# Last stage of a two-layer audio tower: top-2 experts by sorted tiles of rows instead of all eight experts for every token

## The reference

```python
logits = jnp.einsum('bsh,he->bse', x, gate_w) + gate_b
topk_vals, topk_idx = jax.lax.top_k(logits, K)                 # K = 2, E = 8
topk_weights = jax.nn.softmax(topk_vals, axis=-1)
mask = jax.nn.one_hot(topk_idx, E, dtype=topk_weights.dtype)
weights = jnp.einsum('bske,bsk->bse', mask, topk_weights)
h = jax.nn.relu(jnp.einsum('bsh,ehf->bsef', x, w1) + b1)
expert_out = jnp.einsum('bsef,efh->bseh', h, w2) + b2
return jnp.einsum('bseh,bse->bsh', expert_out, weights)
```

## Time and profile before

| what | value |
| --- | --- |
| median of three runs | 2385.1 us (2382.28 to 2393.17) |
| profiled execution, whole | 2387.96 us |
| its span, first to last instruction | 2386.1 us |
| mean granted TensorE clock | 0.944 of full speed |
| busy: PE, DVE, ACT, POOL | 86%, 66%, 45%, 32% |

### The profile page before, as it was taken

The page is one execution under the profiler, slowest core; times in us unless marked ns, Lnnn a source line. Parts: engine busy times, 40 slices in busy tenths (PEclk is TensorE's granted clock), DMA queues, the critical chain, the costliest instruction groups (busy, mean ns, idle before and its releaser), DMA issues. The chain is left out here.

```text
span 2386.1 us, 54761 instructions
## 1 busy us (share of the span) xinstructions
PE 2052.9 (86%) x20986; PEld 1812.3 (76%) x20986; DVE 1563.6 (66%) x3984; ACT 1079.6 (45%) x2700; POOL 769.3 (32%) x730
## 2 busy tenths in 40 slices
PE   6599989998726776786899999994999999999998
PEld 5497778786615676686677777773999999999998
DVE  4745665654743653556699999996666676676664
ACT  4433333422614453452666666662444444444443
POOL 0002222200055424520577777774121121121120
PEclk9899999999858897898999999997999999999999
DMA  7100100100311101100000000000000000000000
GB/s 180 37 1 12 15 11 12 15 1 2 111 42 35 30 20 35 36 16 1 3 3 3 3 3 3 3 3 1 8 8 7 13 7 7 13 7 7 13 7 14
DMA packets 80356, 44.52 MB, mean 19 GB/s; under 512 B 45800, under 2 KB 74024, under 8 KB 79752
## 3 DMA queue, kind: packets, MB, share of 16 engines
q1 hardware_dynamic: 74248, 29.53, 5.4%
q0 software_dynamic: 5888, 12.07, 1.9%
HBM read 27.20 MB, written 14.38 MB: 17 GB/s over the span
## 5 line engine op out<-in xcount | busy, mean ns | idle before, releaser
L2103 ACT ACTIVATE w<-banks,b 128x384 f32<-128x384 f32 (+1 forms) x512 | 259.5, 572 | 392.9 <-PE banks L2177 392.9
L2159 PE MATMUL banks<-w,w 128*128 128x128 f32 (+1 forms) x3072 | 364.1, 275 | 0.0
L2159 PEld LDWEIGHTS banks<-w,w 128*128 128x128 f32 (+1 forms) x3072 | 350.4, 189 | 9.1 <-issue 8.7
L1694 PE MATMUL banks<-qT,w 64*64 64x128 f32 x4608 | 272.2, 271 | 14.9 <-DVE eb L1597 12.3
L1702 PE MATMUL banks<-eb,w 64*64 64x128 f32 x4608 | 272.4, 271 | 0.7 <-DVE eb L1597 0.7
L1694 PEld LDWEIGHTS banks<-qT,w 64*64 64x64 f32 x4608 | 249.3, 133 | 29.8 <-DVE eb L1597 17.0
L2004 DVE SCALAR_TENSOR_TENSOR h<-banks,t_wt,h 128x128 f32 (+3 forms) x672 | 183.9, 343 | 115.1 <-PE banks L2159 112.4
L1702 PEld LDWEIGHTS banks<-eb,w 64*64 64x64 f32 x4608 | 249.2, 133 | 1.3 <-DVE eb L1597 1.1
L1237 POOL DMA_INDIRECT xg<-xs,rowu x184 | 179.2, 974 | 152.3 <-PE banks L1388 90.4
L1662 POOL TENSOR_TENSOR t<-eb 128x768 f32<-128x768 f32 x96 | 175.9, 1832 | 135.8 <-ACT eb L1642 123.7
L1597 DVE TENSOR_TENSOR eb<-eb,rd 128x1536 f32<-128x1536 f32 x96 | 211.7, 2205 | 1.6 <-ACT rd L1651 1.6
(11 more groups left out here) (309 smaller groups left out, 4354.4 us busy)
## 6 DMA issues: line engine op xcount, KB each, us to landing
out<-h SPq DMA_DIRECT2D x16, 320.0 KB
xs<-r_xl SPq DMA_DIRECT2D x16, 192.0 KB, 2.9
h<-in_xT SPq DMA_DIRECT2D x4, 750.0 KB, 15.0
h<-in_xT SPq DMA_DIRECT2D x4, 749.0 KB, 17.9
xg<-xs,rowu POOLq DMA_INDIRECT x184
xs<-r_xl SPq DMA_DIRECT2D x16, 128.0 KB
blocks<-NT SPq DMA_DIRECT2D x24, 48.0 KB, 1.9
D<-blocks SPq DMA_DIRECT2D x24, 48.0 KB, 2.0
```

The source lines that it names most:

```text
L1694: last = nc.tensor.matmul(lbanks(n)[place(n, hd), v, :], k.Kt[half(hd), v, :], qT[half(hd), n // NC % 2, (n % NC) * P:(n % NC + 1) * P], s ...
L2103: nc.scalar.activation(gb[u % 2][:, f, s * GW:s * GW + NFREE[s]], k.ps[:, order.bank(n), 0:NFREE[s]], ACT.Relu, bias=k.b1_1[:, 2 * e + f:2 ...
L2159: last = nc.tensor.matmul(k.psf[0:n, o:o + P], gb[u % 2][:, f, c * P:c * P + n], k.w2_1[:, 2 * e + f, :], start=(f == 0), stop=(f == 1))
```

## The change

`TailOrder` gives way to `TailPlan`, and the tail stage is written out anew, without loops. Per pair of sequences (1492 tokens, 2984 choices):

- The fronts of both sequences of the next pair are done in 15 items (`FRONT`), one in each step of the pair in hand. DVE does them in a fixed order of its own, ending in `places`; the normalisation of the attention's result moves from DVE to ACT (`norm_out`), the products with the norm's parameters move from POOL to DVE (two passes in `norm_sum`), and POOL keeps one addition (`shift`) and the roots.
- `places`: PE counts, by 13 matmuls, how many choices for each expert come ahead of each token; DVE works out from it where in a list sorted by expert each choice goes (each expert begins at a multiple of 128 rows), and which expert owns each of the 31 tiles of 128 rows.
- `send`: POOL writes the normalised tokens to that list in DRAM (`sorted_x`), by 24 indirect transfers (six chunks, two sequences, two choices).
- SP loads the list in eight groups of four tiles (`tiles_in`). PE transposes each tile, ACT evicts it. In 16 steps of two tiles each, ACT copies the owner's first weights for each tile (`own_weights`, a register loaded from SBUF for the address), PE does the hidden matmuls in plain float32, ACT the bias and ReLU per tile and half (62 a pair), PE the output matmuls, with a register load per tile for the second weights. ACT evicts, SP stores to `sorted_y`.
- `fetch`: POOL gathers each token's two results back by 24 indirect transfers, while the next pair is computed and the front of the one after it is done; DVE multiplies them by the two weights and adds them to `h` (`combine`, 24 instructions in place of 96 a pair).

The tail has 31 tiles of 128 rows a pair where every token's eight experts were 11936 rows. Two copies of each list are kept, filled with zeros at the start by SP. The core of the diff, in the order plan, SP, POOL, DVE, ACT, PE:

```diff
-    def pair(self, last_pair):
...
-        for u in range(2 * E1):
-            par, e = divmod(u, E1)
...
-            out += [("hidden", x, u) for x in range(4)]
...
+    FRONT = (("turn_o", 0), ("lin", 0), ("turn_o", 1), ("lin", 1), ("turn_x", 0), ("logits", 0), ("turn_x", 1),
+             ("logits", 1), ("gate", 0), ("gate", 1), ("places", 0), ("wT", 0), ("bias", 0), ("wT", 1), ("bias", 1))
+    TILES = (2 * 2 * T + E1 * (P - 1)) // P
...
+    def experts(self, p):
+
+        out, ahead = [], self.front(p + 1) if p + 1 < PAIRS else []
+        first, steps = p * self.GROUPS, 2 * self.GROUPS
+        out.append(("tiles", first))
+        for s in range(steps):
+            G = first + s // 2
+            if s % 2 == 0 and s // 2 + 1 < self.GROUPS:
+                out.append(("tiles", G + 1))
+            out.append(("hidden", 2 * first + s))
+            out += ahead[s:s + 1]
+            if s:
+                out.append(("output", 2 * first + s - 1))
+        assert len(ahead) <= steps
+        return out + [("output", 2 * first + steps - 1)]
...
+                def tiles_in(G):
+                    p, g = divmod(G, GROUPS)
+                    if g == 0:
+                        sp.wait_ge(sent, SENT * (p + 1))
+                    if G >= 3:
+                        sp.wait_ge(tile_ps, G - 2)
+                    t = order.tiles(g)
+                    sp.dma_start(xs[:, G % 3, 0:len(t), :],
+                                 k.sorted_x[p % 2][t[0] * P:(t[-1] + 1) * P, :].rearrange("(j p) d -> p j d", p=P)
+                                 ).then_inc(tile_in[G % 3], 16)
...
+                def send(p):
+                    pool.wait_ge(placed, p + 1)
+                    pool.wait_ge(normed_x, 4 * (p + 1))
...
+                    for m in range(2 * NC):
+                        n = rows(m % NC)
+                        for j in range(2):
+                            nc.gpsimd.indirect_dma_start(
+                                out=k.sorted_x[p % 2], in_=xl[0:n, m, :], in_offset=None,
+                                out_offset=bass.IndirectOffsetOnAxis(ap=place[0:n, p % 3, j, m:m + 1], axis=0),
+                            ).then_inc(sent, 16)
...
+                for p in range(-1, PAIRS):
+                    ahead, behind = p + 1 < PAIRS, p >= 1
+                    if ahead:
+                        shift(2 * (p + 1))
+                        shift(2 * (p + 1) + 1)
+                        root(2 * (p + 1), 0)
+                    if behind:
+                        fetch_ready(p - 1)
+                    for n, (q, w) in enumerate(((0, 1), (1, 0), (1, 1))):
+                        if behind:
+                            fetch(p - 1, every[3 * n:3 * n + 3])
+                        if ahead:
+                            root(2 * (p + 1) + q, w)
+                    if behind:
+                        fetch(p - 1, every[9:])
+                    if ahead:
+                        if p == -1:
+                            pool.wait_ge(blank, 32)
+                        send(p + 1)
+                fetch_ready(PAIRS - 1)
...
+                    if p + 1 < PAIRS:
+                        b = 2 * (p + 1)
+                        linear_sum(b)
+                        norm_sum(b)
+                        linear_sum(b + 1)
+                        norm_tokens(b)
+                        norm_sum(b + 1)
+                        rank(b)
+                        norm_tokens(b + 1)
+                        weigh(b)
+                        rank(b + 1)
+                        weigh(b + 1)
+                        places(p + 1)
...
+                def own_weights(x):
+                    p, s = divmod(x, HALVES)
+                    act.wait_ge(owned, p + 1)
+                    if x >= 2:
+                        act.wait_ge(h_ps, x - 1)
+                    for j, t in enumerate(order.tiles(s // 2, s % 2)):
+                        e = nc.values_load(ids[0:1, p % 3, t:t + 1], engines=[mybir.EngineType.Activation], min_val=0,
+                                           max_val=E1 - 1)
+                        last = nc.scalar.activation(w1_own[:, x % 2, j, None, :], w1[:, bass.ds(e, 1), :], ACT.Copy)
+                    last.then_inc(w1_ready, 1)
...
+                    elif kind == "output":
+                        p, s = divmod(x, HALVES)
+                        G = x // 2
+                        pe.wait_ge(h_ready, x + 1)
+                        if s % 2 == 0 and G >= 2:
+                            pe.wait_ge(y_ready, G - 1)
+                        for j, t in enumerate(order.tiles(s // 2, s % 2)):
+                            e = nc.values_load(ids[0:1, p % 3, t:t + 1], engines=[mybir.EngineType.PE], min_val=0,
+                                               max_val=E1 - 1)
+                            at = (2 * (x % 2) + j) * P
+                            for f in range(2):
+                                last = nc.tensor.matmul(k.ps[:, 6 + G % 2, None, at:at + C], hid[:, x % 2, j, f, :],
+                                                        w2[:, f, bass.ds(e, 1), :], start=(f == 0), stop=(f == 1))
```

More of the change, by code:

```diff
@@ L1824, in tail_phase @@
-        U = 2 * E1
-        SMALL, RANKS, RANKED = 7, 18, 12
+        zero = sb("t_zero", [P, P])
+        steps = sb("t_steps", [P, 12 + 32 + 64])
+        valid = sb("t_valid", [P, P])
+        onesq = sb("t_ones", [P, P])
+        above = sb("t_above", [P, E1, 12])
+        need, ends, begins = (sb("t_" + x, [P, E1]) for x in ("need", "ends", "begins"))
+        upto = sb("t_upto", [P, E1, E1])
+        spot = sb("t_spot", [P, 2 * NC, E1])
+        spots = sb("t_spots", [P, 2, 2 * NC, E1])
+        placef = sb("t_placef", [P, 2, 2 * NC])
@@ new lines, in norm_tokens @@
+                def norm_tokens(b):
+                    for c in range(NC):
+                        last = nc.vector.bn_stats(stats[:, 1, c, :], k.h[:, b, c, :])
+                    link(last)
+                    variance(b, 1)
+                    if b % 2 == 0 and b:
+                        dve.wait_ge(sent, SENT * (b // 2))
+                    for c in range(NC):
+                        last = nc.vector.tensor_scalar(xl[:, b % 2 * NC + c, :], k.h[:, b, c, :], mean[:, 1, c:c + 1],
+                                                       rstd[:, 1, c:c + 1], ALU.subtract, ALU.mult)
@@ L2127, in fill @@
[L2127 to L2141 removed]
+                pe.wait_ge(wl_ready, 1)
@@ L2147, in fill @@
                                                     k.gate1[:, :], start=True, stop=True)
-                    last.then_inc(full, 1)
-                def output(i, u, last_pair):
-                    e = u % E1
-                    done = max(n for n, (kind, _, v) in enumerate(order.of(last_pair)) if kind == "hidden" and v == u)
-                    pe.wait_ge(free, order.emptied(i, done, False, last_pair))
-                    pe.wait_ge(added, i * U + (u + 1))
-                    for c in range(NC):
-                        n = rows(c)
-                        o = 2048 + (u % 2) * 1024 + c * P
-                        for f in range(2):
-                            last = nc.tensor.matmul(k.psf[0:n, o:o + P], gb[u % 2][:, f, c * P:c * P + n],
-                                                    k.w2_1[:, 2 * e + f, :], start=(f == 0), stop=(f == 1))
-                    last.then_inc(o_ps, 1)
```

718 lines of the change are left out of this document (392 added, 326 removed).

## The result

The changed kernel takes 2685.4 us (median of four runs, 2681.3 to 2691.3); the kernel before took 2388.2 beside it. The ratio is 1.1247, interval 1.1211 to 1.1284. The forecast was 2663, the range 2520 to 2790. The profiled execution took 2691.3, its span is 2689.4. The tail starts at 1645.5 in place of 1640. That is none of the change's doing: the loads of `h` at the start landed after 21.1 and 24.1 us in this trace and after 15.0 and 17.9 in the one before.

The account below looks back on a forecast made before the run. PE throughput bounded the old tail (88.7 us a pair); after the change, a chain through all engines once per pair. Start 1640 + head 93 + 7 periods of 116 + end 119 = 2664 us span, 2663 forecast, range 2520 to 2790.

Parts of the forecast that it names:

- end: Last pair, without a front: 15 steps of 4.5 us, store, 24 gathers, last combine and output, 119 us in all.
- Front, 82.1: Chain of one pair from its first tiles landing through all engines to `placed`: 82.1 us.
- twelve loads on the chain: Register loads for expert weights in a period's chain, priced at 0.8 us each.
- Scatters, 30: After `placed`, POOL's 24 scatters at 1.25 us each lie on the chain: 30.0 us a pair.
- rival of slow scatters: Writes of scattered rows cost POOL 2.0 us each, period 135, total 2833 us; chance 0.08.
- Landing and load, 4: After a pair's last scatter, landing and the tile load that SP holds back for all 24: 4.0 us.
- A step, 4.5: One experts' step of two tiles: 4.5 us, between ACT's mean 4.1 and PE's 3.6 to 6.0.
- Gathers done before: POOL's gathers of a pair end at 72 us in the chain, ahead of `placed` at 82.1.
- The stall for the exponent: DVE, through `norm_tokens` at 55.5 us, stands at `weigh` until ACT's exponent, an item two steps on, at 69.5.
- short chain: Rival: register loads near the low end and PE keeping full clock, 2524 to 2600 us; chance 0.2.
- Long loads: Rival: register loads on PE and ACT cost 1.9 us each in two in-order queues, 2791 us; chance 0.15.
- POOL-bound rival: Fronts and scatters lie wholly beside experts' steps, period is POOL's sum 69.3 us, total 2317; chance 0.04.

Follow-up runs that it names:

- kind A: Runs on chips where the kernel before takes 2384 to 2388 us; the unedited changed kernel takes 2685.4 us there, ratio 1.1247.
- kind B: Runs on chips where the kernel before takes 2279 us; the unedited changed kernel takes 2501.6 us there, ratio 1.0983.
- experiment 6: Changed kernel without its 496 register loads, each tile using a constant expert (tile number modulo 8): 2497.2 us beside 2501.6, ratio 1.0966.
- experiment 1: Changed kernel without the 12 scatters of the second choices of every pair: 2549.5 us, ratio 1.068.
- experiment 7: Changed kernel with order alone altered, the exponent and the counting matmuls queued earlier and places before the second weights: 2460.0 us, ratio 1.0789.
- experiment 9: On top of experiment 7, fronts two pairs ahead of the experts, with a third `sorted_x`: 2394.8 us, ratio 1.0512.
- experiment 10: On top of experiment 9, POOL's `b3n` additions moved to DVE and gathers spread between the roots: 2403.9 us, ratio 1.0545.

## Why the prediction was right, point by point

The sign, the mechanism (a chain through all engines once per pair) and nearly the sum were right. The sum was right on kind A alone, where the prediction's rows come from: on kind B the 2501.6 us lie below the whole range, because 106 us ahead of the tail are gone, and with the start at 1640 they would be some 2604. The sum in the prediction's own terms, with a period counted from first tile to first tile:

| term | predicted | kind A | kind B |
|---|---|---|---|
| start of the tail | 1640 | 1645.5 | 1533.8 |
| head | 93 | 93 | 93 |
| mean of seven periods | 116 | 116.7 | 108.0 |
| end | 119 | 133.9 | 115.2 |
| span | 2664 | 2689.4 | 2498.3 |

**The mean period of 116.7 is a hit that two errors made.** A later period, from last scatter to last scatter, falls apart into three terms:

| term of a later period | predicted | kind A | kind B |
|---|---|---|---|
| first tile to `placed` | 82.1 | 79.0 | 69.3 |
| 24 scatters, from `placed` | 30.0 | 33.3 | 33.3 |
| last scatter to first tile | 4.0 | 6.5 | 6.1 |

On kind A the front was 3 shorter than forecast and the other two terms 3 and 2 longer, and behind those 3 stand a front forecast too long by 13 and gaps of 10. That these came out even is luck.

- *Front, 82.1:* too long by 13 on kind B, where nothing disturbs it. The term that failed is "twelve loads on the chain", 12 x 0.8 = 9.6: they cost nothing there (experiment 6). The step behind it: I priced the load as time in which its engine stands, while the sequencer runs it beside the work ahead. The second linear map also came 8.3 us after the first in place of 12.7. On kind A the gaps put 9.7 us back (79.0 - 69.3), a mechanism that no step named.
- *Scatters, 30:* on the chain, all of them, as forecast (experiment 1). Mis-sized by 3.3, because my row was of full transfers and those of 106 rows take 1.86 in place of 1.25. The rival of slow scatters falls: 128 rows cost 1.26 out as well as in.
- *Landing and load, 4:* 6.1 (kind A's 6.5 is the mean with one of 8.0). From the end of the last scatter to SP's first tile load 3.1, and 3.0 until PE has the tiles.
- *A step, 4.5:* the prices of its parts were right: ReLU 0.37 (368 ns), weight copy 0.4 (0.42), clock between the two levels (0.70 to 0.78). But 4.5 is not the middle of the two prices of PE that I gave, 3.6 and 6.0: that is 4.8. In the end, which has no front beside it, the loads cost 0.36 us a tile where I had 0.8 a load (experiment 6), and a step took 3.9 on kind B. So the first gather there comes 72 us after the first tile where I had 79, and the 119 is near 115.2 because the gathers took 32 for 30 and what follows them 11 for 10. On kind A the gaps make a step 5.2 and the end 133.9.
- *Gathers done before:* they were, on both kinds, and on kind B they cost about 1 us a period. On kind A "done before" was no proof of "costs nothing": 12 us.
- *The stall for the exponent:* there as forecast, up to 13 us a pair on kind B and up to 20.7 on kind A. What it was worth was 6 us a period (experiment 7), since the counting behind it was late too.
- *Rivals:* short chain (2524 to 2600) named cheap loads, and on kind B they were: its tail of 964 us behind the start at 1640 would be 2604, just above this rival's 2600. I gave it 0.2. What I left out was that a sequencer can run ahead of its engine. The other half of it, a PE that keeps its full clock, fell. Long loads fall. The POOL-bound rival needed `placed` by 42; it came at 69. Only experiment 9 gave the chain that slack, and even then the period was 88.3 and not 69.3: POOL's own work, with the time between its transfers, was 76, it waited 12 for DVE, and PE's queue has its own waits (experiment 10).

## What to carry to other kernels

When a change halves the busiest engine, look for the longest loop through all engines, which set the new time here: count it event by event, and check it by taking one link out (half the scatters gave half their time back, 136 us for 134). Leave room in the order before saving work: with fronts two pairs ahead the period fell by 15 us, with no instruction made cheaper. And an experiment that puts other work in the place of a suspect must be read in its own profile, since additions on POOL reproduced the 119 us by another mechanism altogether.

## What the runs showed of the hardware

- While POOL issues indirect transfers, on kind A ACT waits up to 11.7 us for PE's results with no releaser in the profile (123.2 us in 17 such waits of L2213 in seven periods). The traces of three chips of kind B have no such gap over 2 us. Between the changed kernel's two traces lie 112 us ahead of the tail and 79 us in it (1044 against 965). The cause is open.
- An indirect transfer of 106 rows costs POOL 1.56 us and the next starts 1.86 after it; one of 128 rows 0.96 and 1.26. It is so for scatters and gathers and on both kinds of chip.
- A register load from on-chip memory takes 0.30 us on PE and 0.28 on ACT, and it runs beside the work ahead of it on its engine (all 248 of each engine in the trace of kind B). Taking all 496 out gained 4 us of 2502.
- Additions of 448 columns on POOL made DVE's `tensor_scalar` on 128 columns go from 368 to 877 ns on average. Beside gathers it stays at 366 to 368.
